# A decoder layer on one core: query and key projections in tiles of 128 tokens across batch borders

## The reference, cut to what matters

```
x: (8, 224, 512)                      # 8 batches of 224 tokens
x = rmsnorm(tokens) * norm_w
q = x @ Wq;  k, v = split(x @ Wkv)    # 16 heads of 64
q, k = head_rmsnorm(q), head_rmsnorm(k)      # norm over the 64 of each head
sim = 50 * tanh(q k^T / 8 / 50)
out = softmax(sim) @ v;  y = out @ Wo;  x1 = layernorm(x + y)
```

## Time and profile before

| | |
|---|---|
| times of three runs | 1792.01, 1792.96, 1793.77 us (median 1792.96) |
| the profiled execution | 1794.0 us, span of the trace 1792.2 us |
| busy | PE 98%, DVE 78%, ACT 66%, POOL 62% |
| self attention | 0 to about 572 us |
| cross attention | about 572 to 1611 us |
| feed forward | about 1611 us to the end |
| granted TensorE clock | full, except for 6.8 us from 563.5 on and twice later |

### The profile page before, as it was taken

How to read it: one execution, slowest core, us unless ns; L and a number is a source line. 1 busy time by engine, 2 the same in 40 slices (tenths; PEclk the granted TensorE clock), 3 DMA queues, 4 the chain that set the end, 5 groups by cost and what they waited for, 6 DMA issues and landing times.

```text
span 1792.2 us, 37462 instructions
## 1 busy us (share of the span) xinstructions
PE 1749.8 (98%) x13957; PEld 1473.0 (82%) x13957; DVE 1402.9 (78%) x3220; ACT 1184.2 (66%) x2691; POOL 1109.4 (62%) x1250
## 2 busy tenths in 40 slices
PE   8999999999998999999999999999999999989997
PEld 7777777787877999999999999899899899975443
DVE  6777778787888777777777788777777787788886
ACT  6878887766765666666666666656566566665774
POOL 3433445754656586786686655578787778652454
PEclk9999999999999999999999999999999999999999
DMA  6222323111105422432432433414314323525553
GB/s 207 77 67 87 102 77 114 52 32 42 53 22 170 153 87 91 153 99 80 153 102 76 158 104 90 113 49 117 94 59 116 97 64 99 130 49 132 147 133 96
DMA packets 141107, 176.82 MB, mean 99 GB/s; under 512 B 63884, under 2 KB 99088, under 8 KB 140928
## 3 DMA queue, kind: packets, MB, share of 16 engines
q1 hardware_dynamic: 122392, 138.15, 25.8%
q0 software_dynamic: 14656, 28.92, 5.9%
q10 hardware_dynamic: 3880, 7.35, 1.4%
HBM read 109.25 MB, written 50.46 MB: 89 GB/s over the span
## 4 chain that ended last, share of the span: by engine, by line
PE 77%; DVE 8%; POOL 5%; DMA 4%; ACT 3%; issue 2%; ACTq 0%; DVEq 0%; POOLq 0%
PE att_ps_T L552 6%; PE att_ps_P L1736 5%; PE att_ps_SA L1760 5%; PE att_ps_SB L612 4%; PE att_ps_P L1724 4%; PE att_ps_P L552 4%; PE att_ps_P L1788 4%; PE att_ps_SB L600 3%; PE att_ps_O L1724 3%; PE att_ps_T L1724 3%; DMA ca_ct<-ct_kept 3%; PE att_ps_T L1736 3%; PE att_ps_P L1774 2%; PE att_ps_SA L2470 2%; PE att_ps_O L1736 2%; PE att_ps_P L1799 2%
## 5 line engine op out<-in xcount | busy, mean ns | idle before, releaser
L1542 POOL TENSOR_TENSOR ca_pr<-ca_pr,ca_rec 112x750 f32<-112x750 f32 x256 | 366.7, 1453 | 181.9 <-DVE ca_rec L2022 179.0
L423 POOL TENSOR_TENSOR sa_p_lo<-sa_pr,sa_p_hi 112x448 fp32r<-112x448 f32 x128 | 146.7, 1160 | 208.6 <-ACT sa_p_hi L718 207.7
L1907 ACT ACTIVATE ca_big<-att_ps_P 126x384 fp32r<-126x384 f32 (+1 forms) x254 | 105.3, 449 | 64.5 <-PE att_ps_P L1774 62.5
L1901 ACT ACTIVATE ca_pr<-att_ps_SA,ca_nmax 112x750 f32<-112x750 f32 x128 | 113.5, 887 | 17.7 <-DVE ca_nmax L2018 6.8
L2027 DVE TENSOR_TENSOR ca_big<-att_ps_P,ca_big 126x384 fp32r<-126x384 f32 (+1 forms) x254 | 120.1, 501 | 5.6 <-ACT ca_big L1907 5.3
L887 DVE RECIPROCAL sa_sums<-sa_sums 128x224 f32<-128x224 f32 x64 | 99.1, 1548 | 31.2 <-ACT sa_sums L727 30.9
L2018 DVE TENSOR_REDUCE ca_nmax<-att_ps_SA 112x1 f32<-112x752 f32 x128 | 119.3, 932 | 1.2 <-PE att_ps_SA L1760 1.2
L2018 DVE TENSOR_REDUCE ca_nmax<-att_ps_SB 112x1 f32<-112x752 f32 x128 | 119.3, 932 | 0.0
L1736 PE MATMUL att_ps_P<-ca_w_hi,ca_ct 128*126 128x256 f32 x558 | 113.9, 283 | 0.0
L1901 ACT ACTIVATE ca_pr<-att_ps_SB,ca_nmax 112x750 f32<-112x750 f32 x128 | 113.0, 883 | 0.2 <-DVE ca_nmax L2018 0.2
L1774 PEld LDWEIGHTS att_ps_P<-att_ident,ca_pr 64*126 64x126 f32 (+1 forms) x1524 | 85.6, 138 | 13.5 <-issue 8.9
(11 more groups left out here) (365 smaller groups left out, 6608.5 us busy)
## 6 DMA issues: line engine op xcount, KB each, us to landing
ct_kept<-ca_ct SPq DMA_DIRECT2D x8, 1134.0 KB, 9.1
ca_ct<-ct_kept POOLq DMA_DIRECT2D x8, 1134.0 KB, 8.2
ct_kept<-ca_ct SPq DMA_DIRECT2D x8, 1116.0 KB, 12.5
ca_ct<-ct_kept POOLq DMA_DIRECT2D x8, 1116.0 KB, 10.3
sa_xin<-in_x_dram SPq DMA_DIRECT2D x16, 448.0 KB, 3.8
xt_kept<-ca_xt SPq DMA_DIRECT2D x8, 896.0 KB, 5.2
ca_xt<-xt_kept POOLq DMA_DIRECT2D x8, 896.0 KB, 5.1
ternary<-ca_stage SPq DMA_DIRECT2D x36, 172.0 KB, 1.9
```

Of the source, the lines that this page charges most:

```text
L423: pool.tensor_tensor(p_lo[:, h % NB, :], pr[:, h % NB, :], f32(p_hi[:, h % NB, :]), ALU.subtract).then_inc(p_split, 1)
L1542: pool.tensor_tensor(w, w, rec[:, h % PB, c:c + 1].to_broadcast([R, S]), ALU.mult).then_inc(norm_done, 1)
L1901: act.activation(pr[:, h % PB, c, :].rearrange("r (a s) -> r a s", a=2), two_halves(psum[slot]), ACT.Exp, bias=nmax[:, h % PB, c:c + 1], a ...
L1907: act.activation(weights_view(h, c, x, False), blocks_view(source.bank, x), ACT.Copy).then_inc(t_hi_done, 1)
```

## The change

The projection of q and k, their norms and their transposes no longer go by halves of 112 tokens but by tiles of P = 128 tokens, counted through over the batches. Four batches (896 tokens) are seven tiles: the batches whose number is 0, 1 or 2 modulo 4 project two tiles each, and every fourth (numbers 3, 7, 11, 15; they are projected in steps 2, 6, 10 and 14) projects one. In detail:

- `xt_hi/xt_lo` and `q_hi/q_lo/k_hi/k_lo` become rings of two batches, and x is loaded and transposed one batch earlier (AHEAD 2 to 3). Values still go by halves of 112.
- Every norm and scale instruction on q and k has 128 rows, not 112.
- Where a batch's tiles cross the ring's end (`RING_PIECES`, numbers 1, 5, 9, 13), each hi and lo part of q and k is written in two pieces, 192 and 64 columns. For numbers 2, 6, 10, 14 one more piece of x is written behind the ring's end (`wraps`).
- The sums of squares of a row must move from a batch's rows to a tile's rows: SP copies them with three or four tiny transfers per batch (`spread_squares`), and the lower bound becomes an instruction of its own, `U` (`guards`), at another place in DVE's order. Both are there for the first 8 numbers only.
- Steps with one tile have orders of their own on PE, ACT and DVE, `WITH_ONE_TILE`: V0 uses the bank that Q1 leaves; on DVE the lo part of V0 stands between the reciprocals `I2` and `I3`; on ACT the hi part of V0 stands behind `B3`. The weight split 4 of group 1 moves on ACT from behind K1 to behind V0 (step 6).
- At the start x[1] is loaded into y's buffer ahead of the weights, and both x[0] and x[1] are transposed before the weights come.
- `th` has two buffers instead of four, `sq` two instead of four.
- In the last steps, the stores of the numbers 13 and 14 stand behind the cross attention's first loads on SP (before, only 14 did). DVE's last layer norm `E14` is done in two halves.
- In the cross attention POOL's load of `ca_ct` is two names, `KC0` and `KC1`, and for the order of group 1 `KC0` stands ahead of `N4.0`.

```diff
-    AHEAD = 2
+    AHEAD = 3
+    PERIOD = 4
+    XW = 2 * N + HALF
+    TILES_IN = PERIOD * N // P
+    TILE_COLUMNS = [[0, P], [2 * P, 3 * P], [HALF, HALF + P], [2 * P + HALF]]
+    TILES_OF = [[0, 1], [2, 3], [4, 5], [6]]
+    RING_PIECES = [[(0, 0, 2 * P)], [(0, 2 * P, P + HALF), (P + HALF, 0, HALF)], [(0, HALF, 2 * P)], [(0, 2 * P + HALF, P)]]
...
     def sync(sp):
+        def spread_squares(m):
+            if m:
+                sp.wait_ge(ss_spread, spread_count(m - 1))
+            for c, r, n, t, row in pieces_of(m):
+                sp.dma_start(tile_ss[row:row + n, t:t + 1], ss[r:r + n, m % 2, c:c + 1]).then_inc(ss_spread, 16)
...
         load_rows(x[0], None)
+        sp.dma_start(y[:, :, :], x[1].rearrange("(c r) n -> r c n", r=R)).then_inc(x_in_second, 16)
         load_weights(0, range(2))
...
         def last_but_one():
+            store(GROUPS - 1, B - 3)
             store(GROUPS - 1, B - 2)
...
         def project(u, at, arriving=False):
 
             i, c = "QKV".index(u[0]), int(u[1])
+            if u[0] != "V" and c >= len(tiles(at)):
+                return
...
+            if u[0] == "V":
+                rows, col = R, ring_at(at) + c * R
+            else:
+                rows, col = P, TILE_COLUMNS[number(at) % PERIOD][c]
...
-                mm = pe.matmul(ps(u)[0:R, :], xs[:, k, c * R:c * R + R], ws[i][:, k, :],
+                mm = pe.matmul(ps(u, at)[0:rows, :], xs[:, k, col:col + rows], ws[i][:, k, :],
...
+        WITH_ONE_TILE = steps("""S1 O0 O1 S2 Q0+ O2 O3 S3 K0+ Q1+ K1+ O4 O5 V0+ O6 O7 V1+ T0+ T1+ Y0 S0+ T2+ Y1 T3+ X+++""")
...
+        WITH_ONE_TILE = steps("""A2 A3 E2 E3 P2 B0 P3 A4 A5 E4 P4 E5 P5 B1 Q0+ A6 A7 E6 K0+ Q1+ K1+ P6 E7 P7 B2 X+++ W0 L B3 V0+ C3 V1+ W1
+                                 W2 T0+ T1+ A0+ T2+ E0+ A1+ P0+ E1+ P1+ T3+ XT0+++ XT1+++""")
...
-        NEXT_SPLITS = {"K1": (4, range(KC)), "W2": (5, range(3)), "T0": (5, range(3, KC))}
+        NEXT_SPLITS = {"V0": (4, range(KC)), "W2": (5, range(3)), "T0": (5, range(3, KC))}
...
-            dve.tensor_scalar(guard[:, :], ss[:, :], 1e-24 / DM, 1e-24 * RMS_EPS, ALU.mult, ALU.add).then_inc(rows_done, 1)
...
+        def guards(at):
+
+            m = number(at)
+            if m >= B:
+                return
+            ready = TILES_READY[m % PERIOD]
+            of = slice(TILES_IN * (m // PERIOD) + ready[0], TILES_IN * (m // PERIOD) + ready[-1] + 1)
+            dve.wait_ge(ss_spread, spread_count(m))
+            dve.tensor_scalar(guard[:, of], tile_ss[:, of], 1e-24 / DM, 1e-24 * RMS_EPS, ALU.mult, ALU.add).then_inc(guard_done, 1)
...
+        FIRST_PART = """D1 HK0+ N0.0+ N0.1+ N0.2+ N0.3+ N0.4+ N0.5+ N0.6+ N0.7+ N0.8+ N0.9+ N0.10+ N0.11+ Q0+ K0+ HQ1+ HK1+ N1.0+
+                        K1a+ Q1a+ Q1b+ K1b+ I2 V0+ D2 I3 U++ V1+ T0+ T1+ Y0 """
...
-                           N2.0+ N3.0+ FT2 N2.1+ N3.1+ L B0+ N4.0+ N5.0+ KC"""),
+                           N2.0+ N3.0+ FT2 N2.1+ N3.1+ L B0+ KC0 N4.0+ KC1 N5.0+"""),
```

349 lines of the change are left out of this document (232 added, 117 removed).

## The result

The changed kernel takes 1813.1 us (median of 4 runs, 1811.2 to 1818.6), the kernel before on the same chips 1793.4. The ratio is 1.011 with a 95% interval of 1.0088 to 1.0131. I had forecast 1787.0 and a range to 1795.5: the time lies outside it, and on the other side of no change.

What follows compares the result with a forecast made beforehand. PE was taken to set the pace, with ACT tight at each step's end. Gains of 16.0 us less losses of 10.05 left 5.95 off the profiled 1794.0, and 1.04 for the runs' median: 1787.0, range 1777 to 1795.5.

Steps and rivals of the forecast that it cites:

- The cross attention: Cross attention: `KC0` ahead of `N4.0` removes PE's waits for `ca_ct`, a gain of 3.5 us, between 0 and 4.0.
- The border to the cross attention: Step 14 and the border: 4.6 us left to gain, less 1.6 for the late store of number 13, gains 3.0.
- The start: Start: x[1] ahead of the weights, extra transposes and parts, row squares and a wrap lose 3.5 us, between 1 and 6.
- Step 2: One-tile step in group 0: 27.8 us of PE work plus a 1.8 wait for `o_split` make 29.6, gaining 4.6.
- Steps 6 and 7: Group 0's end: 6.4 us less the 1.8 wait and 1.7 for ACT's moved weight split, gaining 2.9.
- Step 10: One-tile step in group 1: 4.35 us lost, as x's transpose waits for a bank DVE frees late; gains 2.0.
- The double pieces: Parts of q and k written in two pieces in four steps: 0.6 us a step, 2.4 lost in all.
- A two-tile step's transposes and projections: Two-tile steps: wider transposes lose 0.22 us in each of 12 steps, 2.6 in all; wider projections cost nothing.
- The lower bound `U`: DVE, path of the inverse roots: `U` costs 0 to 0.75 us in five steps, 0.8 lost together.
- rival 4: Self attention: `U` held up by POOL, 2.54 us in five steps, 12 us worse, 1799; chance 0.05.
- Rival 3: Half clock also falls at the new waits of steps 2, 6, 10 and 14: 13.6 us, 1800.6; chance 0.06.
- Rival 2: Waits at `o_split`, the late store and double pieces at upper bounds eat the gain: no change, about 1793; chance 0.22.

Runs made afterwards that it cites:

- experiment 2: The kernel before, with only the split context load (`KC0` ahead of `N4.0`) added: median 1807.1 us, ratio 1.0075 to the kernel before.
- experiment 5: The changed kernel with the context load as before and store 13 between the cross attention's first x load and its weights: median 1794.6 us, ratio 1.0008.
- experiment 4: The changed kernel with 2 instead of 22 idle matmuls ahead of the first projection: median 1812.4 us, ratio 1.0099 to the kernel before.
- experiment 10: On top of experiment 5, the lower bound `U` of number 1 computed ahead of the weights' lo parts in the fill: median 1793.7 us.
- experiment 9: On top of experiment 5, ScalarE's row squares of x[2] moved behind the hi part of V0 in the fill: median 1793.9 us, ratio 0.9994.
- experiment 12: Experiment 5 with the edits of experiment 9 and experiment 10 together: median 1792.0 us, ratio 0.9989 to the kernel before.
- experiment 11: On top of experiment 5, both halves of the context load between `N4.0` and `N5.0` in the cross attention's group 1: median 1802.2 us, ratio 1.0038.
- experiment 3: The changed kernel with store 13 ahead of the cross attention's context loads on SyncE: median 1817.7 us, ratio 1.0144 to the kernel before.
- experiment 7: The changed kernel with the context load as before and, in one-tile steps, V0's lo part behind the last reciprocal: median 1799.9 us, ratio 1.0039.
- experiment 13: On top of experiment 12, ScalarE's weight split 4 in step 6 put back to K1's place: median 1795.2 us, ratio 1.0007.
- experiment 14: On top of experiment 12, in one-tile steps `O6 O7` ahead of V0 on TensorE and V0's lo part behind the last reciprocal on VectorE: median 1796.7 us.
- experiment 8: The changed kernel with GpSimd's `FR2 B3` turned to `B3 FR2` in group 1 of the cross attention: median 1808.1 us, ratio 1.0079.

## Why the prediction was wrong, by its steps

**The cross attention is the step that failed.** I wrote that `KC0` ahead of `N4.0` "issues that load before POOL's 2.8 us of normalisation", took +3.5 and the range 0 to 4.0. It is -13.6 in the trace and -13 in experiment 2, 17 of the 26 us between forecast and result. The border makes about 6 of them and the start another 6; the steps were 2 better than forecast. I had asked what waits for the load, and not what is issued with it: the feed-forward weights on SyncE, for which GpSimd waits in order, and behind which its split stands. The lower bound of 0 had no row behind it. About a quarter of the price is half clock behind the new waits (6.7 us of it, 3.4 lost). None of my rivals named this; it is a transfer that shifts another transfer.

**The border to the cross attention.** I took +3.0 with a price of 0 to 2.7 for the late store. The store landed 6.0 us after its issue at 547.17 and VectorE waited 8.4; with the clock the stretch lost 2.9. Experiment 5 gives 6.8 us back by moving that one store, 5.2 of them at the border in its trace, and then the stretch gains 2.5, near the 3.0 that I had. So the price was of the right place and too small: it left out that the transfer itself has 2.6 MB ahead of it in the queue (6.0 us to land against 3.4 with the weights behind it), and the half clock behind TensorE's wait.

**The start.** Forecast 3.5, between 1 and 6; measured 6.7 to the end of the fill and 3.2 in step 0. The parts: the first projection at 14.1 instead of 11.0 us, since the idle matmuls stand behind x[1]'s transposes (experiment 4); 1.3 us of `U` beside GpSimd's weight parts (experiment 10), which I had priced in the steps and not in the fill; and ScalarE's squares ahead of the first tanh (0.8 to 1.7 us, experiment 9), forecast at 1.2. The rest is half clock, which went only when the last two were mended together (experiment 12). One part of it is in the kernel before too: in experiment 2, whose start is that of the kernel before, half clock came at 37 to 40 us, and its first projection started at 9.0 instead of 11.0. The trace of before that I read had none, though the same two waits of TensorE (0.7 and 1.2 us) stand in both. So some 1 to 3 us of this loss is one execution against another.

**The steps, as forecast.** Steps 1 to 12 gave 6.2 us; by my terms 4.6 + 2.9 + 2.0 of gain less some 5.1 of loss is 4.4. Step 2: 4.8 (forecast 4.6). Steps 6 and 7: 2.0 in the changed trace, with half clock behind the 2.1 us of wait that I had priced at 1.7. Step 10: 3.0 (forecast 2.0). The wait there is, as said, ahead of x's transposes and released by VectorE, but 1.4 us long and not 2 to 3. The double pieces cost less than forecast: step 4, which has them, is 0.24 us longer than before, and steps 1 and 5, which have none, 0.4. Steps 8 and 12 are 0.8 longer with them, but so is step 9 without; in group 1 something else costs some 0.4 us in three steps, which I did not follow. A two-tile step's transposes and projections cost what I took: about 109 ns a transpose instead of 95, and matmuls 233 ns apart instead of 231, where I had said that the width costs nothing; that is 0.1 us a step more.

**The lower bound `U`.** Its median is 0.16 us where it stands now, 1.29 at most, in the fill. There it began 0.04 us behind an instruction of GpSimd (29.36 us) and ended with it. That fits the rule of the Trainium skill (SBUF — State Buffer, "SBUF: two separate sides") that VectorE or GpSimd, whichever starts first, holds the port pair that they share for its whole instruction and blocks the other. Moved ahead of GpSimd's work `U` took 0.16 (experiment 10). In the steps each of its six rows starts just as an instruction of GpSimd has ended, so they cost nothing and don't test the rule. So rival 4 did not come. I had misread the row of 2.54 us, too: it does not end with the pair of the earlier trace rows, at 278.69, but at 279.72, with the first of the two that follow on GpSimd:

```profile
278.64 2.05 POOL L447 TENSOR_TENSOR sa_w_hi<-sa_ff_in,sa_wnorm 128x512 fp32r<-128x512 f32 x2
```

**The rivals.** Rival 3 named the clock as what could make it slower, with a wrong count: it fell at one of the four waits named (step 6), did not fall in steps 2 and 10, and fell at the border and in the cross attention, which have the long waits. The clock is thus a part of their price and of the start's, not a term of its own. Rival 2 (the waits eat it all) is nearest for the self attention as a whole: +6.7 + 3.2 - 6.2 + 2.9 leaves it 6.7 us behind. Experiment 12 shows what it can be: 3.7 us ahead of the kernel before at the first context product of the cross attention, in one trace.

**What stays open.** Why experiment 12 is not further ahead: by the marks it is 3.7 us ahead at 575 us and 1.1 at the feed forward in its one trace, with a wait of 1.5 us for `ca_o_lo` in the cross attention that the kernel before has not. I did not follow this. Nor is it shown why the half clock at the start went with the edits of experiments 9 and 10 together and stayed with each alone. That the feed-forward load is slow because of the context load just ahead of it rests on five traces that agree (6.5 and 6.6 us when it is issued 0.9 us behind the first half, 9.0 and more when it is issued further behind both); how the queues share the transfers was not looked at.

## What to carry to other kernels

When a transfer is issued earlier, list what else is issued around it and who waits for that: here a load that TensorE waited 4 us for, issued 1.4 us earlier, cost 7.6 us (experiment 11), and with its halves some 3 and 2 us earlier 13 (experiment 2), through a smaller load behind it and an engine that works in order. A store for which an engine waits must not stand behind a large load that nobody needs yet; put the small transfer that is waited for ahead of it, and leave alone the loads that are already early (experiments 3 and 5). Removing a projection gave what it costs less a new wait, and in experiments 7, 13 and 14 moving instructions only moved the waits to other places without making the whole faster; I take the chain over VectorE and GpSimd to be the bound of such a step, which no run shows. Two short waits close together can be worth mending at once where mending either changes nothing (experiments 9, 10 and 12).

## What the runs showed of the hardware

- At the lower of TensorE's two levels a matmul of 512 columns takes 0.43 us (573.40 to 573.83 us of the changed kernel, granted clock 0.50), at the higher one 0.23.
- In the cross attention, where single waits stand between long full stretches, half clock followed each of ten waits of 1.8 to 3.2 us in four traces (the changed kernel, experiments 2, 8 and 11), some 3.4 us of it each time, and none of those of 0.6 to 1.6 us. In the self attention waits of 1.4 us in full stretches (steps 2 and 10) brought none; at the start, where several of 0.4 to 2.3 us stand together, it came in eleven traces with tiles and stayed away in the three in which two of them are shortened.
- The fill of one and the same self attention, the kernel before's, differs by 2.1 us between two traces (end of the fill at 36.9 and 34.8 us), since its 22 idle matmuls started 213 ns apart until nearly 11 us in one and 112 from about 7 us on in the other. The Trainium skill (TensorE: Matmul & The Clock Gate, "Part 1: The HAM clock gate") states that the point of the rise varies between runs, by 500 ns either way. That it varies these two traces show, but by some 4 us.
- 344 KB issued 0.9 us behind the first of two loads of 1.1 MB, and together with the second, was usable after 6.6 us; issued 4.2 us behind the first and 1.9 behind the second, after 9.3; issued 2.3 and 1.4 us behind them, after 9.0 (experiment 11).
- A store of 448 KB landed 6.0 us after its issue with 2.6 MB of loads ahead of it on the same queue, and after 3.4 us with them behind it (experiment 5).
